# Two-layer graph network on one core: attention probabilities turned by transposing DMA transfers instead of TensorE transposes, with a new bank table and a new order of the work

## The chip, the cores and the metric

The kernel runs on one core of a Trainium2 chip. The time is device microseconds (us) from one launch to its end. Three runs of the kernel before gave 1729.15, 1730.36 and 1730.51 us, so the median is 1730.36 us. All times below are in us unless marked ns.

## The reference, cut to what matters

The input is 64 graphs of 128 nodes with 384 features each, and a weighted adjacency matrix per graph. Two residual blocks follow each other. Everything is float32.

```python
h = maximum(layernorm(x), 0)
# block 1: attention with 12 heads of 32 features, adj added twice to the scores
q, k, v = h @ Wq.T, h @ Wk.T, h @ Wv.T + bv             # per head
scores = einsum('bqhd,bkhd->bhqk', q, k) * 384**-0.5 + (adj + adj)
scores = where(any(scores != 0, -1), scores, -inf)
p = nan_to_num(softmax(scores))
x = x + einsum('bhqk,bkhd->bqhd', p, v) @ Wo.T + bo
# block 2: two layers of a gated graph convolution on h = maximum(layernorm(x), 0)
u = (h @ (h@Wl.T).T) * triu(adj) / sqrt(384) + (h @ (h@Wr.T).T) / sqrt(384) * triu(adj, 1).T
d = exp(u) * adj;  h = relu(layer_norm(d / sum(d) @ (h @ Wlin.T + b)))
x = x + h
```

## The kernel before, in words

Two graphs form a group, so there are 32 groups (`g`, NG = 32) and 256 tokens in a group. Every operand of a large product is kept as a high part and a low part (`HI`, `LO`); a product of two such operands is three matmuls. The high part is written by ScalarE (`hi`, line 480) when it drains a PSUM bank, and the low part by VectorE (`lo`, line 592), which subtracts the high part from the same bank.

The work of a group is cut into named jobs. For the attention: `T1a/T1b` turn the normed input, `QK0..2` and `V0/V1` project, `S{j}{c}` computes the scores of graph `j` for the four heads of chunk `c`, `x{j}{c}` is the exponential, `P{j}{c}` turns the probabilities, `PV{j}` multiplies them with the values, `OT{j}` turns the result and `WO{j}` is the output projection. For the graph layers `l` = 0, 1: `T2a/T2b`, `N{l}{k}` and `HL{l}{j}` project, `U{l}` is the pair product, `C{l}{j}` the aggregation, `HTa/HTb` turn the hidden state between the layers, and `AT` turns the adjacency matrix. There is one table `ORDER` with a fixed list of steps for each engine (lines 82 to 110), run once per turn of the loop. The number beside a step says how many groups ahead it works, so that a turn mixes steps of several groups. `BANK` (lines 71 to 80) says which of the 8 PSUM banks a job fills. Each engine runs its list strictly in order; waits on semaphores (`wait_filled`, `wait_drained`) tie the lists together.

The part that changes is the way of the probabilities. Before, VectorE adds the adjacency to the scores and takes the row maximum in one instruction per head (line 655), writes minus twice the maximum (`m{j}{c}`, line 662), and ScalarE takes the exponential into `prob` (line 509). TensorE then turns four heads into a bank (line 420), ScalarE writes the high part of `pT` (float16) from the bank and VectorE the low part (line 597). `PV` (line 413) reads `pT` as its stationary operand. Before, `prob` has room for both graphs of a group; `pT` has room for one graph.

q and k are restacked through SyncE's DMA queue (line 301): 12 transfers for q and 12 for k in each turn. The masks of the two triangles come from products with constant triangles: the left one on VectorE from the bank of `AT` (line 705), the right one on GpSimd (line 836). GpSimd also applies the last scale and shift of the output (`za`, `zb`, lines 840 and 843) and adds the bias `bo` (`xbo`, line 832). VectorE's step `U{l}` is a chain: `m` multiplies with the masks (line 721), `w` adds the two sides (line 724), `d` multiplies with the turned adjacency (line 727), `dh` and `dl` split (lines 730 and 733), and `C{l}{j}` on TensorE waits for `dl`.

Of the kernel before, what the change touches and what calls it, by code (L numbers as in the profile page):

```python
# [61 lines left out]
def w_lin(l):  # L62
# [9 lines left out]
    0: ["QK2", "N11", "HL11", "C10", "N01", "P10"],  # L72
    1: ["PV1", "OT1", "V0", "U1", "S12", "P01", "P11"],
    2: ["T1b", "QK0", "T2b", "S02", "S11", "P02", "AT"],
    3: ["C01", "HTb", "V1", "P00", "U0"],
    4: ["WO0", "HTa", "N12", "T2a", "S00", "N00", "P12"],
    5: ["WO1", "S10", "HL00"],
    6: ["OT0", "T1a", "QK1", "HL10", "N02", "PV0"],
    7: ["HL01", "C00", "N10", "S01", "C11"],
# [4 lines left out]
        ("out", -2), ("q3", 1), ("ld_x", 2), ("k3", 1), ("ld_adj", 2)],  # L84
# [6 lines left out]
    "ACT": [  # L91
# [6 lines left out]
    "DVE": [  # L98
# [9 lines left out]
    "POOL": [  # L108
        ("za", -2), ("zb", -2), ("xbo", 1), ("gn0", -1), ("ln2", 0), ("ln1", 2), ("ml", 0), ("gn1", -1)],
# [3 lines left out]
SPLIT_JOBS = (["T1a", "T1b", "QK0", "QK1", "QK2", "V0", "V1"] + [f"P{j}{c}" for j in range(G) for c in range(C)] +  # L113
              ["OT0", "OT1", "T2a", "T2b", "AT"] + [f"N{l}{k}" for l in range(L) for k in range(3)] +
# [6 lines left out]
def build(nc, x_d, adj_d, w_d, bias_d, bo_d, lna_d, lnb_d, out_d):  # L121
# [17 lines left out]
    with ExitStack() as ctx:  # L139
# [13 lines left out]
        upper = sb("upper", [P, P])  # L153
        lower = sb("lower", [P, P])
# [16 lines left out]
        prob = sb("prob", [P, G, NH, P])  # L171
# [4 lines left out]
        rmax = sb("rmax", [P, G, NH])  # L176
        nmax = sb("nmax", [P, G, NH])
# [47 lines left out]
        s_mr = sem("mask_right")  # L225
# [7 lines left out]
        s_za, s_zb, s_y = sem("scaled"), sem("shifted"), sem("result")  # L233
# [107 lines left out]
        def _(pe):  # L341
# [39 lines left out]
            def run(step, g):  # L381
# [24 lines left out]
                elif step[:2] == "PV":  # L406
                    j = int(step[2])
                    wait_drained(pe, f"V{j}", g)
                    for c in range(C):
                        wait_drained(pe, f"P{j}{c}", g)  # L410
# [63 lines left out]
        def _(act):  # L474
# [12 lines left out]
            def run(step, g):  # L487
# [17 lines left out]
                elif step[0] == "x" and len(step) == 3:  # L505
                    j, c = int(step[1]), int(step[2])
                    act.wait_ge(s_max[j][c], g + 1)
# [3 lines left out]
                elif step[0] == "P":  # L511
                    j, c = int(step[1]), int(step[2])
# [363 lines left out]
```

## Time and profile before

| what | value |
|---|---|
| median of 3 runs | 1730.36 us |
| the profiled execution itself | 1729.59 us |
| its span, first to last instruction | 1727.8 us |
| TensorE busy | 1590.1 us (92%) |
| VectorE busy | 1283.4 us (74%) |
| ScalarE busy | 922.7 us (53%) |
| GpSimd busy | 450.8 us (26%) |
| mean granted TensorE clock | 0.966 |
| chain that ended last | TensorE 50%, VectorE 26%, ScalarE 13% |

Busy time is an average over the whole span. TensorE is busy in nearly all of it, yet VectorE and ScalarE are on half of the chain that ended last, because the lists of the four engines wait for each other several times in a turn. Which engine limits a stretch has to be read from that stretch.

### The profile page before, as it was taken

To read this page: it belongs to the slowest core of one execution; us is meant where nothing else is said; L and a number is where in the kernel's file an instruction comes from. 1 tells how busy PE (TensorE), PEld (TensorE's weight loads), DVE (VectorE), ACT (ScalarE), POOL (GpSimd) and SP (SyncE) were. 2 spreads that over 40 slices of the span, in tenths; PEclk is the share of its full clock that TensorE was granted. 3 is DMA by queue.
4 is the path that set the end of the run, shared out by engine and by line. 5 is a ranking of instruction groups with operands and counts; after the bars stand their busy time and mean duration, and the time that the engine had idled before them with its cause. 6 is when DMAs were issued, how large, how long until landed. Compare 5 with 4: busy or idle time off the path is not lost.

```text
span 1727.8 us, 39233 instructions
## 1 busy us (share of the span) xinstructions
PE 1590.1 (92%) x13888; PEld 1542.7 (89%) x13888; DVE 1283.4 (74%) x4495; ACT 922.7 (53%) x2155; POOL 450.8 (26%) x804
## 2 busy tenths in 40 slices
PE   4699999999999999999999999999999999999974
PEld 3599999999999999999999999999999999999974
DVE  5567877778887778787777887777788777787752
ACT  3455565455556456556455555545565645555531
POOL 4112321222222232222132232123222223223121
PEclk8799999999999999999999999999999999999996
DMA  6111111211112111111111111111111112111100
GB/s 202 38 36 26 43 41 47 50 49 29 36 41 50 47 50 41 28 45 41 47 50 47 29 39 41 50 47 50 38 30 45 41 47 50 44 29 41 29 10 18
DMA packets 116767, 76.16 MB, mean 44 GB/s; under 512 B 14282, under 2 KB 116432, under 8 KB 116576
## 3 DMA queue, kind: packets, MB, share of 16 engines
q1 hardware_dynamic: 116128, 73.06, 16.6%
q8 instruction: 114, 1.87, 0.5%
q14 instruction: 77, 0.63, 0.1%
q0 software_dynamic: 448, 0.60, 0.1%
HBM read 23.28 MB, written 12.58 MB: 21 GB/s over the span
## 4 chain that ended last, share of the span: by engine, by line
PE 50%; DVE 26%; ACT 13%; issue 6%; SPq 4%; DMA 1%; POOL 1%; POOLq 0%; ACTq 0%; DVEq 0%
PE bank L344 45%; ACT prob L509 6%; DVE prob L655 6%; SPq L301 4%; DVE pT L597 3%; DVE dT L730 3%; DVE work L724 3%; ACT pT L485 3%; ACT n L485 3%; DVE hl L597 2%; PE bank L350 2%; ACT c_sb L541 2%; DVE work L721 1%; DVE stats_gnn L630 1%; DVE rmax L655 1%
## 5 line engine op out<-in xcount | busy, mean ns | idle before, releaser
L344 PE MATMUL bank<-h,weights 128*128 128x256 f32 x3456 | 438.4, 284 | 5.8 <-DVE h L746 5.1
L344 PEld LDWEIGHTS bank<-h,weights 128*128 128x128 f32 x3456 | 420.3, 190 | 6.9 <-issue 5.7
L509 ACT ACTIVATE prob<-prob,nmax 128x128 f32<-128x128 f32 x768 | 236.2, 405 | 71.0 <-DVE nmax L662 71.0
L344 PE MATMUL bank<-hA,weights 128*128 128x256 f32 x1728 | 228.7, 292 | 1.5 <-DVE hA L597 1.5
L344 PEld LDWEIGHTS bank<-hA,weights 128*128 128x128 f32 x1728 | 223.6, 201 | 2.0 <-issue 2.0
L344 PE MATMUL bank<-weights,h 128*128 128x384 f32 x1152 | 224.6, 339 | 0.0
L597 DVE TENSOR_TENSOR n<-bank,n 128x512 fp32r<-128x512 f32 x192 | 131.4, 685 | 113.9 <-ACT n L485 113.7
L485 ACT ACTIVATE qk<-bank 128x512 f16<-128x512 f32 x96 | 57.3, 597 | 270.0 <-PE bank L344 269.9
L344 PEld LDWEIGHTS bank<-weights,h 128*128 128x128 f32 x1152 | 195.6, 188 | 0.0
L485 ACT ACTIVATE n<-bank 128x512 fp32r<-128x512 f32 x192 | 116.3, 606 | 120.2 <-PE bank L344 120.2
L655 DVE CUSTOM_DVE_ANT_0 prob<-bank,adj_sb 128x128 f32<-128x128 f32 x768 | 174.0, 287 | 0.9 <-issue 0.8
L812 POOL TENSOR_SCALAR less_mean_gnn<-mv_gnn 128x2 f32<-128x2 f32 x64 | 14.1, 220 | 556.7 <-DVE mv_gnn L602 556.7
L344 PE MATMUL bank<-n,h 128*128 128x256 f32 x1152 | 153.6, 287 | 0.0
L344 PE MATMUL bank<-hl,dT 128*128 128x386 f32 x384 | 91.2, 377 | 63.2 <-DVE dT L733 60.9
L344 PEld LDWEIGHTS bank<-n,h 128*128 128x128 f32 x1152 | 141.9, 191 | 0.2 <-issue 0.2
L799 POOL TENSOR_SCALAR less_mean_ln<-mv_ln 128x2 f32<-128x2 f32 x64 | 14.1, 220 | 481.0 <-DVE mv_ln L602 481.0
L485 ACT ACTIVATE hl<-bank 128x384 fp32r<-128x384 f32 x128 | 63.9, 499 | 141.1 <-PE bank L344 141.1
L597 DVE TENSOR_TENSOR pT<-bank,pT 128x512 f16<-128x512 f32 x192 | 126.0, 684 | 14.0 <-ACT pT L485 13.2
L344 PEld LDWEIGHTS bank<-hl,dT 128*128 128x128 f32 x384 | 70.2, 204 | 72.4 <-issue 72.4
L344 PE MATMUL bank<-weights,hA 128*128 128x384 f32 x576 | 115.2, 344 | 2.7 <-DVEq L587 2.7
L344 PE MATMUL bank<-weights,oT 128*128 128x384 f32 x576 | 115.9, 346 | 1.8 <-DVE oT L597 1.8
L420 PE MATMUL bank<-ident,prob 128*128 128x128 f32 x768 | 109.2, 280 | 1.8 <-ACT prob L509 1.7
(112 smaller groups left out, 2874.6 us busy)
## 6 DMA issues: line engine op xcount, KB each, us to landing
q<-qk SPq DMA_DIRECT2D x384, 48.0 KB, 1.9
k<-qk SPq DMA_DIRECT2D x384, 48.0 KB, 2.0
x_sb<-x SPq DMA_DIRECT2D x32, 384.0 KB, 3.5
out<-x SPq DMA_DIRECT2D x32, 384.0 KB, 2.5
adj_sb<-adj SPq DMA_DIRECT2D x32, 128.0 KB, 2.1
prob<-w SPq DMA_DIRECT2D x4, 576.0 KB, 6.4
x<-w SPq DMA_DIRECT2D x3, 576.0 KB, 4.6
pT<-w SPq DMA_DIRECT2D x3, 576.0 KB, 6.1
```

The lines of the kernel that those rows point to most:

```text
L301: sp.dma_start(dst[D * r:D * r + D, a:NH:HC, :], qk[D * a:D * a + D, part, first:first + C, :]).then_inc(s, 16)
L344: mm = pe.matmul(out, lhsT, rhs, start=(n == 0), stop=(n == len(pairs) - 1))
L350: mm = pe.transpose(bank(job)[:, n * T + j * P:n * T + (j + 1) * P], src[:, j, c * P:(c + 1) * P], ident[:, :])
L420: mm = pe.transpose(bank(step)[:, a * P:(a + 1) * P], prob[:, j, c * HC + a, :], ident[:, :])
L485: act.activation(out, src, ACT.Copy).then_inc(s_hi, 1)
L509: e = act.activation(prob[:, j, h, :], prob[:, j, h, :], ACT.Exp, bias=nmax[:, j, h:h + 1], scale=2.0)
L541: act.activation(c_sb[:, j, :], bank(f"C1{j}")[:, 0:H], ACT.Copy).then_inc(free(f"C1{j}"), 1)
L597: dve.tensor_tensor(out, src, hi_part if hi_part.dtype == F16 else hi_part.bitcast(F32), ALU.subtract).then_inc(free(job), 1)
L630: dve.bn_stats(stats["gnn"][:, j, :], bank(f"C{l}{j}")[:, 0:H]).then_inc(s_gst[l][j], 1)
L655: r = dve.tensor_tensor_reduce(prob[:, j, h, :], bank(step)[:, a * P:(a + 1) * P], adj_sb[:, p, j, :], 1.0, -3.0e38, ALU.add, ALU.max, rma ...
L724: dve.tensor_tensor(wu, tu[:, :, 0, :], tu[:, :, 1, :], ALU.add).then_inc(s_w[l], 1)
L730: dve.tensor_copy(dT[:, HI, :, :], wu).then_inc(s_dhi[l], 1)
```

## The change

1. The `P` jobs leave TensorE. ScalarE copies `prob` from SBUF into a new float16 tile `pp` (named `prob_parts` in the profile; steps `ph`), VectorE writes the low part (`pl`), and 12 transposing DMA transfers per turn on SyncE's queue write `pT` from it (steps `pth` and `ptl`: high and low, graph `j`, chunk `c`). `prob` now has room for one graph only, and `pp` as well.
2. The row maximum is taken as a minimum of minus twice the sum, so that the `m` steps go.
3. `AT` is drained by ScalarE alone, and both masks are made on GpSimd by `affine_select` (steps `mu`, `ml`).
4. `za`, `zb`, `xbo` and `y` are cut into one step per graph.
5. `BANK` and `ORDER` are new. The loop now runs up to three groups ahead instead of two.

```diff
 BANK = {
-    0: ["QK2", "N11", "HL11", "C10", "N01", "P10"],
+    0: ["C00", "S02", "S01", "N01"],
...
     "SP": [
-        ("out", -2), ("q3", 1), ("ld_x", 2), ("k3", 1), ("ld_adj", 2)],
+        ("pth12", 1), ("ptl12", 1), ("ptl11", 1), ("pth11", 1), ("pth10", 1), ("ptl10", 1), ("ld_adj", 2), ("out", -1),
+        ("q3", 2), ("ld_x", 3), ("k3", 2), ("pth02", 2), ("ptl02", 2), ("pth00", 2), ("pth01", 2), ("ptl01", 2), ("ptl00", 2)],
...
-        prob = sb("prob", [P, G, NH, P])
+        prob = sb("prob", [P, NH, P])
+        pp = sb("prob_parts", [P, 2, NH, P], F16)
         pT = sb("pT", [P, 2, NH, P], F16)
...
+                elif step[:2] == "pt":
+                    part, j, c = "hl".index(step[2]), int(step[3]), int(step[4])
+                    hs = slice(c * HC, (c + 1) * HC)
...
+                    sp.wait_ge(s_part[part][c], G * g + j + 1)
+                    if j == 0:
+                        wait_filled(sp, "PV1", g - 1)
+                    else:
+                        wait_filled(sp, "PV0", g)
+                    sp.dma_start_transpose(pT[:, part, hs, :], pp[:, part, hs, :].rearrange("p h q -> p (h q)")).then_inc(s_turned[part][c], 16)
...
                 elif step[:2] == "PV":
...
-                    for c in range(C):
-                        wait_drained(pe, f"P{j}{c}", g)
+                    for part in (HI, LO):
+                        for c in range(C):
+                            pe.wait_ge(s_turned[part][c], 16 * (G * g + j + 1))
...
-                elif step[0] == "P":
-                    j, c = int(step[1]), int(step[2])
-                    pe.wait_ge(s_exp[j][c], g + 1)
-                    for a in range(HC):
-                        mm = pe.transpose(bank(step)[:, a * P:(a + 1) * P], prob[:, j, c * HC + a, :], ident[:, :])
...
-                        e = act.activation(prob[:, j, h, :], prob[:, j, h, :], ACT.Exp, bias=nmax[:, j, h:h + 1], scale=2.0)
+                        e = act.activation(prob[:, h, :], prob[:, h, :], ACT.Exp, bias=rmin[:, j, h:h + 1], scale=-1.0)
...
+                elif step[:2] == "ph":
...
+                    act.wait_ge(s_exp[j][c], g + 1)
+                    ge(act, s_turned[HI][c], 16 * (G * g + j))
+                    act.activation(pp[:, HI, hs, :], prob[:, hs, :], ACT.Copy).then_inc(s_part[HI][c], 1)
...
-                        r = dve.tensor_tensor_reduce(prob[:, j, h, :], bank(step)[:, a * P:(a + 1) * P], adj_sb[:, p, j, :],
-                                                     1.0, -3.0e38, ALU.add, ALU.max, rmax[:, j, h:h + 1])
+                        r = dve.tensor_tensor_reduce(prob[:, h, :], bank(step)[:, a * P:(a + 1) * P], adj_sb[:, p, j, :],
+                                                     -2.0, 3.0e38, ALU.add, ALU.min, rmin[:, j, h:h + 1])
...
-                    dve.tensor_scalar(nmax[:, j, hs], rmax[:, j, hs], -2.0, None, ALU.mult).then_inc(s_max[j][c], 1)
...
+                elif step[:2] == "pl":
...
+                    dve.wait_ge(s_part[HI][c], G * g + j + 1)
+                    ge(dve, s_turned[LO][c], 16 * (G * g + j))
+                    dve.tensor_tensor(pp[:, LO, hs, :], prob[:, hs, :], pp[:, HI, hs, :], ALU.subtract).then_inc(s_part[LO][c], 1)
...
-                    dve.tensor_tensor(mask[:, :, 0, :], bank("AT")[:, 0:T].rearrange("p (g i) -> p g i", g=G),
-                                      upper[:, :].unsqueeze(1).to_broadcast([P, G, P]), ALU.mult).then_inc(free("AT"), 1)
...
+                elif step == "mu":
...
+                    pool.affine_select(out=mask[:, :, 0, :], in_=adjT[:, :, :], compare_op=ALU.is_ge, fill=0.0, base=0,
+                                       pattern=[[0, G], [-1, P]], channel_multiplier=1).then_inc(s_mask[0], 1)
```

TensorE, from the last scores of a turn to the first pair product `U0` (`n2,h0`), before. Rows with `ident,prob` are the `P` jobs, `v2,pT` is `PV0`, `ident,adj_sb` is `AT`:

```order
L404 MATMUL bank5<-k3,q3 128x128 x4
L420 MATMUL bank1<-ident,prob 128x128 x4
L420 MATMUL bank2<-ident,prob 128x128 x4
L344 MATMUL bank0<-h0,weights 128x256 x18
L344 MATMUL bank5<-weights,h0 128x384 x9
L344 MATMUL bank5<-bias_rows,pick 128x384
L413 MATMUL bank6<-v2,pT 128x33 x36
L420 MATMUL bank1<-ident,prob 128x128 x4
L438 MATMUL bank2<-ident,adj_sb 128x128 x2
L420 MATMUL bank4<-ident,prob 128x128 x4
L420 MATMUL bank0<-ident,prob 128x128 x4
L344 MATMUL bank3<-n2,h0 128x256 x18
```

And now, up to the row ahead of the second `v2,pT` (`ident,o_sb` is `OT0`, the second `weights,h0` is `HL01`, `ident,qk` is `T1a` and `T1b`, `weights,oT` is `WO0`):

```order
L416 MATMUL bank1<-k3,q3 128x128 x4
L356 MATMUL bank3<-weights,h0 128x384 x9
L356 MATMUL bank3<-bias_rows,pick 128x384
L426 MATMUL bank5<-v2,pT 128x33 x36
L445 MATMUL bank1<-ident,adj_sb 128x128 x2
L356 MATMUL bank6<-n2,h0 128x256 x18
L433 MATMUL bank2<-ident,o_sb 128x128 x3
L356 MATMUL bank4<-weights,h0 128x384 x9
L356 MATMUL bank4<-bias_rows,pick 128x384
L362 MATMUL bank6<-ident,qk 128x128 x4
L362 MATMUL bank7<-ident,qk 128x128 x2
L356 MATMUL bank1<-weights,oT 128x384 x9
```

The row behind it is `L426 MATMUL bank3<-v2,pT 128x33 x36`, `PV1`. The `P` jobs are gone, `HL00` (`weights,h0`) still stands before `PV0`, and between `U0` and `PV1` there are now `T1a`, `T1b` and `WO0` as well, which stood behind `PV1`.

The order of SyncE's DMA queue over one turn, with what each row waits for, before (`full` and `free` are the filled and drained counts of a bank):

```order
L301 DMA q3<-qk 32x3x256 [waits full2,full1,full5,free6,free2,full7,full4]
L301 DMA q3<-qk 32x3x256 x11
L308 DMA x_sb<-x 128x2x384 [waits free5,free4]
L301 DMA k3<-qk 32x3x256 [waits full2,full1,full5,free6,free0,full7,full4]
L301 DMA k3<-qk 32x3x256 x11
L315 DMA adj_sb<-adj 128x2x128 [waits free2,free1,free5,full2,mask_right,free7,free4]
L329 DMA out<-x1 128x2x384 [waits result]
```

And now, where `full3` is the bank of `PV1` and `full5` the bank of `PV0`:

```order
L300 DMA k3<-qk 32x3x256 x11
L337 DMA_TRANSPOSE pT<-prob_parts 128x4x128 [waits full3,prob_hi2]
L337 DMA_TRANSPOSE pT<-prob_parts 128x4x128 [waits full3,prob_lo2]
L337 DMA_TRANSPOSE pT<-prob_parts 128x4x128 [waits full3,prob_hi0]
L337 DMA_TRANSPOSE pT<-prob_parts 128x4x128 [waits full3,prob_hi1]
L337 DMA_TRANSPOSE pT<-prob_parts 128x4x128 [waits full3,prob_lo1]
L337 DMA_TRANSPOSE pT<-prob_parts 128x4x128 [waits full3,prob_lo0]
L337 DMA_TRANSPOSE pT<-prob_parts 128x4x128 [waits full5,prob_hi2]
L337 DMA_TRANSPOSE pT<-prob_parts 128x4x128 [waits full5,prob_lo2]
```

Four more transposing transfers with `full5` follow, and then `ld_adj`. So the six transfers of the second graph can start only when TensorE has finished `PV0`, and the six of the first graph only when it has finished `PV1` of the group before.

## Rows read from the trace of the kernel before

**Rows 1.** TensorE's waits, whole run: engine, line, releaser; total, times, longest.
```profile
PE bank L344 <- DVE dT L733: 60.9, 31, 4.1
```
**Rows 2.** Windows: length, then busy by engine, PEclk, DMA share, GB/s.
```profile
802.17:854.26 52.09, 49.99 (x437) 48.69 (x435) 39.77 (x141) 28.37 (x68) 13.64 (x24) 0.97 0.16 41
852.00:864.00 12.00, 12.00 (x119) 11.61 (x116) 11.53 (x76) 9.89 (x29) 0.00 (x0) 1.00 0.01 2
823.90:826.00 2.10, 2.09 (x7) 2.10 (x8) 2.10 (x6) 0.00 (x0) 0.00 (x0) 0.53 0.03 8
```
**Rows 3.** Timeline of TensorE: first scores of four turns (start, length).
```profile
134.06 0.62 PE L404 MATMUL bank<-k,q 96*128 96x128 f16 x8
...
851.64 0.62 PE L404 MATMUL bank<-k,q 96*128 96x128 f16 x8
...
1055.06 0.62 PE L404 MATMUL bank<-k,q 96*128 96x128 f16 x8
...
1107.13 0.62 PE L404 MATMUL bank<-k,q 96*128 96x128 f16 x8
```
**Rows 4.** Timeline of TensorE from the P jobs to PV1, one turn.
```profile
857.11 0.61 PE L420 MATMUL bank<-ident,prob 128*128 128x128 f32 x4
857.48 1.30 PE L344 MATMUL bank<-hl,dT 128*128 128x386 f32 x6
...
858.85 1.04 PE L420 MATMUL bank<-ident,prob 128*128 128x128 f32 x8
859.65 2.38 PE L344 MATMUL bank<-h,weights 128*128 128x256 f32 x18
...
863.61 1.07 PE L413 MATMUL bank<-v,pT 128*128 128x33 f16 x36
864.53 0.64 PE L420 MATMUL bank<-ident,prob 128*128 128x128 f32 x4
...
866.01 2.40 PE L344 MATMUL bank<-n,h 128*128 128x256 f32 x18
...
870.32 1.07 PE L413 MATMUL bank<-v,pT 128*128 128x33 f16 x36
```
**Rows 5.** Timeline of TensorE behind PV1, an early turn.
```profile
104.83 1.07 PE L413 MATMUL bank<-v,pT 128*128 128x33 f16 x36
105.75 0.85 PE L350 MATMUL bank<-ident,qk 128*128 128x128 f32 x6
106.36 1.83 PE L344 MATMUL bank<-weights,oT 128*128 128x384 f32 x9
108.03 1.21 PE L344 MATMUL bank<-hl,dT 128*128 128x386 f32 x6
```
**Rows 6.** Timeline of ScalarE: exponentials, then a copy of four heads.
```profile
854.12 3.63 ACT L509 ACTIVATE prob<-prob,nmax 128x128 f32<-128x128 f32 x12 [1.49 <-DVE nmax L662]
857.76 0.60 ACT L485 ACTIVATE pT<-bank 128x512 f16<-128x512 f32 x1
```
**Rows 7.** Timeline of VectorE: two additions of U's chain, the last split before U0.
```profile
817.53 1.68 DVE L724 TENSOR_TENSOR work<-work 128x256 f32<-128x256 f32 x1
...
850.90 0.42 DVE L724 TENSOR_TENSOR work<-work 128x256 f32<-128x256 f32 x1
...
864.10 0.69 DVE L597 TENSOR_TENSOR n<-bank,n 128x512 fp32r<-128x512 f32 x1
```
**Rows 8.** Timeline of SyncE's queue: start, length.
```profile
813.46 0.37 SPq L315 DMA_DIRECT2D adj_sb<-adj  x1
...
832.83 7.66 SPq L301 DMA_DIRECT2D q<-qk  x12
```
**Rows 9.** DMA: a queue with its packets; an issue with us to landing.
```profile
q1 hardware_dynamic: 116128, 73.06, 16.6%
q<-qk SPq DMA_DIRECT2D x384, 48.0 KB, 1.9
```
**Rows 10.** Timeline of GpSimd: scale, shift and bias of the output.
```profile
817.10 1.84 POOL L840 TENSOR_TENSOR c_sb<-c_sb,lna_all 128x768 f32<-128x768 f32 x1 [2.44 <-ACT c_sb L552]
```

More of the change, by code:

```diff
@@ L71 @@
 BANK = {
-    0: ["QK2", "N11", "HL11", "C10", "N01", "P10"],
[L73 to L79, printed above, removed]
+    0: ["C00", "S02", "S01", "N01"],
+    1: ["AT", "WO0", "HTa", "V0", "HL10", "S00", "S12", "S10"],
+    2: ["OT0", "QK0", "N10", "N00"],
+    3: ["PV1", "OT1", "WO1", "U1", "C11", "HL00"],
+    4: ["HL01", "QK1", "V1", "HL11", "C10"],
+    5: ["C01", "T2a", "S11", "PV0"],
+    6: ["U0", "T1a", "HTb", "N11"],
+    7: ["T1b", "QK2", "N12", "T2b", "N02"],
 }
@@ L83 @@
     "SP": [
-        ("out", -2), ("q3", 1), ("ld_x", 2), ("k3", 1), ("ld_adj", 2)],
[2 rows of a table added]
     "PE": [
[5 rows of a table removed]
-    "ACT": [
[6 rows of a table removed]
-    "DVE": [
[9 rows of a table removed]
[4 rows of a table added]
+    "ACT": [
[6 rows of a table added]
+    "DVE": [
[8 rows of a table added]
     "POOL": [
-        ("za", -2), ("zb", -2), ("xbo", 1), ("gn0", -1), ("ln2", 0), ("ln1", 2), ("ml", 0), ("gn1", -1)],
-}
-SPLIT_JOBS = (["T1a", "T1b", "QK0", "QK1", "QK2", "V0", "V1"] + [f"P{j}{c}" for j in range(G) for c in range(C)] +
-              ["OT0", "OT1", "T2a", "T2b", "AT"] + [f"N{l}{k}" for l in range(L) for k in range(3)] +
+        ("mu", 0), ("za1", -1), ("za0", -1), ("zb1", -1), ("zb0", -1), ("xbo0", 2), ("gn0", 0), ("xbo1", 2), ("ln2", 1),
+        ("ml", 1), ("ln1", 3), ("gn1", 0)],
+}
+SPLIT_JOBS = (["T1a", "T1b", "QK0", "QK1", "QK2", "V0", "V1",
+              "OT0", "OT1", "T2a", "T2b"] + [f"N{l}{k}" for l in range(L) for k in range(3)] +
               [f"HL{l}{j}" for l in range(L) for j in range(G)])
@@ L215, in build @@
         s_xn2 = [sem(f"xn2_{j}") for j in range(G)]
-        s_xbo = sem("x_plus_bo")
+        s_xbo = [sem(f"x_plus_bo{j}") for j in range(G)]
         s_q3, s_k3 = sem("q3_in"), sem("k3_in")
-        s_max = [[sem(f"row_max{j}{c}") for c in range(C)] for j in range(G)]
         s_exp = [[sem(f"exps{j}{c}") for c in range(C)] for j in range(G)]
+        s_part = [[sem(f"prob_{n}{c}") for c in range(C)] for n in ("hi", "lo")]
+        s_turned = [[sem(f"prob_turned_{n}{c}") for c in range(C)] for n in ("hi", "lo")]
         s_stats = {k: sem(f"stats_{k}") for k in ("ln1", "ln2")}
@@ L232, in build @@
         s_h1lo = {ab: sem(f"h1_lo_{ab}") for ab in "ab"}
-        s_za, s_zb, s_y = sem("scaled"), sem("shifted"), sem("result")
+        s_za, s_zb, s_y = ([sem(f"{n}{j}") for j in range(G)] for n in ("scaled", "shifted", "result"))
         s_out = [sem("out0"), sem("out1")]
@@ L243, in build @@
         SPLIT_AFTER = {
-            "ACT": {"": (0,), "xn1_1": (1,), "T1a": (2, 3), "QK0": (4, 5), "QK1": (6,), "QK2": (7,), "V0": (8,), "V1": (9,)},
-            "DVE": {"ln1_ag": (0,), "T1a": (1, 2), "QK0": (3, 4), "QK1": (5,), "QK2": (6, 7), "V0": (8,), "V1": (9,)}}
+            "ACT": {"": (0,), "xn1_1": (1,), "T1b": (2, 3), "QK0": (4, 5), "QK1": (6,), "QK2": (7,), "V0": (8,), "V1": (9,)},
+            "DVE": {"ln1_ag": (0,), "T1b": (1, 2), "QK0": (3, 4), "QK1": (5,), "QK2": (6, 7), "V0": (8,), "V1": (9,)}}
         def staged(m):
-            prob_flat = prob[:, :, :, :].rearrange("p g h q -> p (g h q)")
             flat = (x1[:, :, :, :].rearrange("p k g h -> p (k g h)")[:, 0:C * H],
                     pT[:, :, :, :].rearrange("p s h q -> p (s h q)").bitcast(F32)[:, 0:C * H],
-                    prob_flat[:, 0:C * H], prob_flat[:, NH * P:NH * P + C * H])[STAGE_OF[m]]
+                    prob[:, :, :].rearrange("p h q -> p (h q)")[:, 0:C * H],
+                    pp[:, :, :, :].rearrange("p s h q -> p (s h q)").bitcast(F32)[:, 0:C * H])[STAGE_OF[m]]
             return flat.rearrange("p (c o) -> p c o", c=C)
@@ L526, in run @@
                     ge(act, s_d[1], g)
-                    hi(step, g, adjT[:, :, :], T, "p (g i) -> p g i", g=G)
+                    wait_filled(act, "AT", g)
+                    act.activation(adjT[:, :, :], bank("AT")[:, 0:T].rearrange("p (g i) -> p g i", g=G), ACT.Copy).then_inc(free("AT"), 1)
                 elif step[0] == "N":
@@ L717, in run @@
                     if step[3:] == "m":
-                        wait_drained(dve, "AT", g)
-                        dve.wait_ge(s_mr, g + 1)
+                        for side in range(2):
+                            dve.wait_ge(s_mask[side], g + 1)
                         wait_filled(dve, job, g)
@@ L733, in run @@
                         dve.tensor_tensor(dT[:, LO, :, :], wu, dT[:, HI, :, :].bitcast(F32), ALU.subtract).then_inc(s_dlo[l], 1)
[L734 to L737 removed]
+                elif step[0] == "y":
+                    j = int(step[1])
+                    dve.wait_ge(s_zb[j], g + 1)
+                    dve.scalar_tensor_tensor(out=x1[:, p, j, :], in0=c_sb[:, j, :], scalar=0.0, in1=x1[:, p, j, :],
+                                             op0=ALU.max, op1=ALU.add).then_inc(s_y[j], 1)
                 elif step[:2] == "HT":
@@ L828, in run @@
                     gnn_scale(int(step[2]), g)
-                elif step == "xbo":
-                    for j in range(G):
-                        pool.wait_ge(s_xn1[j], g + 1)
-                    pool.tensor_tensor(x_sb[:, p, :, :], x_sb[:, p, :, :], bo_all[:, :].unsqueeze(1).to_broadcast([P, G, H]), ALU.add).then_inc(s_xbo, 1)
+                elif step[:3] == "xbo":
+                    j = int(step[3])
+                    pool.wait_ge(s_xn1[j], g + 1)
+                    pool.tensor_tensor(x_sb[:, p, j, :], x_sb[:, p, j, :], bo_all[:, :], ALU.add).then_inc(s_xbo[j], 1)
+                elif step == "mu":
+                    wait_drained(pool, "AT", g)
+                    wait_drained(pool, "U1", g - 1)
+                    pool.affine_select(out=mask[:, :, 0, :], in_=adjT[:, :, :], compare_op=ALU.is_ge, fill=0.0, base=0,
+                                       pattern=[[0, G], [-1, P]], channel_multiplier=1).then_inc(s_mask[0], 1)
                 elif step == "ml":
@@ L835, in run @@
                     wait_drained(pool, "U1", g - 1)
-                    pool.tensor_tensor(mask[:, :, 1, :], adj_sb[:, p, :, :], lower[:, :].unsqueeze(1).to_broadcast([P, G, P]), ALU.mult).then_inc(s_mr, 1)
-                elif step == "za":
-                    for j in range(G):
-                        pool.wait_ge(s_z[j], g + 1)
-                    pool.tensor_tensor(c_sb[:, :, :], c_sb[:, :, :], lna_all[:, :].unsqueeze(1).to_broadcast([P, G, H]), ALU.mult).then_inc(s_za, 1)
-                elif step == "zb":
-                    pool.wait_ge(s_za, g + 1)
-                    pool.tensor_tensor(c_sb[:, :, :], c_sb[:, :, :], lnb_all[:, :].unsqueeze(1).to_broadcast([P, G, H]), ALU.add).then_inc(s_zb, 1)
+                    pool.affine_select(out=mask[:, :, 1, :], in_=adj_sb[:, p, :, :], compare_op=ALU.is_ge, fill=0.0, base=-1,
+                                       pattern=[[0, G], [1, P]], channel_multiplier=-1).then_inc(s_mask[1], 1)
+                elif step[:2] == "za":
+                    j = int(step[2])
+                    pool.wait_ge(s_z[j], g + 1)
+                    pool.tensor_tensor(c_sb[:, j, :], c_sb[:, j, :], lna_all[:, :], ALU.mult).then_inc(s_za[j], 1)
+                elif step[:2] == "zb":
+                    j = int(step[2])
+                    pool.wait_ge(s_za[j], g + 1)
+                    pool.tensor_tensor(c_sb[:, j, :], c_sb[:, j, :], lnb_all[:, :], ALU.add).then_inc(s_zb[j], 1)
             for step, g in program("POOL"):
```

55 lines of the change are left out of this document (18 added, 37 removed), and 38 rows, old and new, of the table ORDER.

## The prediction

> **What bounds the kernel now.** I read the windows first. In a turn of 52.09 us TensorE is busy 49.99, VectorE 39.77 [rows 2], so TensorE comes first. Then its waits: all that counts is one wait a turn, 31 times, 60.9 us in all, for the last step of VectorE's chain `U0` (`dl`) [rows 1], some 1.95 us each. The starts of the first scores show the turns: 14 turns from 134.06 to 851.64, so 51.26 us on average, and one of 52.07 [rows 3]. A turn of 52.07 has a slow stretch behind that wait: from 823.90 on the granted clock is 0.53, half of full speed, that is 1.2 GHz against 2.4, after TensorE stood idle [rows 2]. If such turns alternate with others, the others take 2 x 51.26 - 52.07 = 50.45 us, and the drop costs 1.6.
>
> Third, the windows by stage. From 852 to 864, the stretch of the scores and the `P` jobs, VectorE is busy 11.53 of 12.00 us [rows 2]. TensorE shows 12.00 there too, but work taken from TensorE alone in this stretch uncovers VectorE at once. Fourth, VectorE's timeline: the same addition of 256 columns takes 1.68 us at 817.53 and 0.42 at 850.90 [rows 7]. At the first place GpSimd runs its scaling, 1.84 us from 817.10 [rows 10].
>
> The Trainium skill has a rule for this (SBUF — State Buffer, "SBUF: two separate sides", on the shared port pair): a VectorE instruction with two SBUF inputs and a GpSimd instruction that reads SBUF exclude each other. By that rule, the trace agrees: 1.68 against 0.42. The rule speaks against this change, because each new `pl` has two SBUF inputs where the old low part read a bank.
>
> **What goes from TensorE.** From the first scores of a turn to `PV0` are 863.61 - 851.64 = 11.97 us [rows 3, 4]. In it the four turnings take 857.48 - 857.11 = 0.37 and the eight 859.65 - 858.85 = 0.80. Between `PV0` and `U0` stand 14 turnings in 866.01 - 864.53 = 1.48 us, 12 of them `P`: 1.27 [rows 4]. Together 2.44 us a turn, 78 us over 32 turns. That is the gain if TensorE bounds all along and nothing new waits.
>
> What is left for TensorE in a turn of the new order, without any wait:
> - first scores to `PV0`: 11.97 - 0.37 - 0.80 = 10.80.
> - `PV0` to `PV1`: 870.32 - 863.61 - 1.27 = 5.44 as before; the new order puts `T1` (106.36 - 105.75 = 0.61) and `WO0` (108.03 - 106.36 = 1.67) [rows 5] in front of `PV1` too, so 7.72.
> - `PV1` to the next first scores: 134.06 - 104.83 = 29.23 [rows 3, 5], less the same 0.61 and 1.67, so 26.95.
>
> Sum 45.5 us. With `U0`'s wait and the slow clock gone as well, this is the floor.
>
> **What goes and comes on the others.** VectorE: the low parts stay six per turn at 512 columns; I price `pl` as the old one, 0.69 us as for the split of that size [rows 7], at most 1.68 - 0.42 = 1.26 more where GpSimd holds it up. In the scores' stretch there now stand four of them where three stood, against six small `m` steps removed; I take that as even. Then VectorE still finishes the last split ahead of `U0` at 864.10 + 0.69 - 851.64 = 13.2 us after the first scores [rows 3, 7], while TensorE, without `P` jobs, would start `U0` at about 10.80 + 0.92 (864.53 - 863.61) + 0.21 for `AT` = 11.9. So 1.3 of the 2.44 us turn into a wait for VectorE, and the floor is 46.8, say 47. The product for the left mask moves to GpSimd and `za`, `zb`, `xbo`, `y` are only cut in two: nothing of them is on this path, GpSimd being busy 13.64 of 52.09 [rows 2]. If that cover is gone they cost up to a microsecond or so a turn; I price it at 0 to 1.
>
> **The new wait.** This is the term that decides. Six transposing transfers fill `pT` for the first graph, then `PV0`; only when TensorE has filled `PV0`'s bank may the next six start, then `PV1`. They sit on one queue and run in order. Let t be the time that one occupies the queue, and t + 1.3 from the issue of the last to its landing (the q copies: 1.9 to landing, of which 7.66 / 12 = 0.64 is the issue [rows 8, 9]). The first can be issued when eight exponentials and one copy are done: the 12 take 3.63 us and the copy 0.60 [rows 6], so 2.4 + 0.6 behind the first exponential, which I put 1.5 after the first scores, earlier than today's 854.12 - 851.64 = 2.5, since it no longer waits for the second chunk and `m`. That is 4.5. Then:
> - `PV0` starts at 4.5 + 5t + t + 1.3 = 5.8 + 6t, if that is over 10.8.
> - `PV1` starts at that + 0.92 + 6t + 1.3 = 8.0 + 12t.
> - the turn is 26.95 more: 35.0 + 12t, if that is over 47.
>
> Behind the waiting `PV1` stand `QK0`, `C01`, `C00` and `QK1` on TensorE, and on VectorE `PV1.r` stands ahead of `dh` and `dl`, which `C01` needs: nothing passes it. On the queue `q3` waits for `QK1` anyway, so it is not delayed further; it moves with `PV1`.
>
> The trace shows no transposing transfer, so t is bounded by the nearest rows. Each moves 128 x 512 float16, 128 KB. Low: the adjacency load, also 128 KB, occupies the queue 0.37 us [rows 8]. High: a q copy has 96 rows of 512 bytes in 0.64 us; a transposing transfer reads 512 rows of 256 bytes, at the same rate 3.4 us. Between them: by the mean packet of the queue, 0.166 x 16 x 1727.8 / 116128 = 39.5 ns [rows 9], 512 packets over 16 engines take 1.26 us; by bytes, q copies move 48 KB in 0.64 us, so 128 KB take 1.7 us. I take 1.7: the q copies are the nearest row, SBUF to SBUF, float16 and on the same queue. It gives `PV0` at 16.0 (5.2 us of waiting), `PV1` at 28.4 where TensorE is free at 16.0 + 7.72 = 23.7 (4.7 us), and a turn of 55.4. Both waits are longer than the one that lets the clock fall today; at 1.6 a drop, 0 to 3.2 a turn, I take 1.7. Turn: 57.1.
>
> The Trainium skill (Advanced Engine Details and Errata, "X-Bar Transpose (TRN2)") says that transposing transfers are as fast as regular ones. No run here shows it yet. By it t would be the issue time, the fast case below. Another page (VectorE: DVE Perf Modes, "The three transpose paths") gives 1309 ns for one 128x128 block; four of them one behind the other would be an estimate of 5.2 us, and a turn of 97.
>
> **Sum.** The ends of the run stay: 1727.8 - 31 x 51.26 = 139 us. 31 x 57.1 + 139 = 1909, and 1.8 around the span gives 1911. The profiled execution of before (1729.59) lies 0.8 under the median, nothing here. I forecast 1910 us, 10% slower.
>
> **Rivals.**
> - *The transfers are hidden* (t up to 1.0; the other side). The turn is 47 to 47.5: 31 x 47.3 + 141 = 1607, 7% faster. For it: a load of the same bytes occupies the queue 0.37 us, and the 16 engines are 84% idle [rows 2]. The page on transposes as fast as copies says the same. Against it: the q copies need 0.64 for 48 KB. It decides below t = 1.3, where 35.0 + 12t with some of the clock's price meets 51.26. 25%.
> - *Nearly even, gaining a little or nothing* (t of 1.0 to 1.35, the estimate by packets): at 1.26 the turn is 50.1, with one clock drop in part 51: 31 x 51 + 141 = 1722. 15%.
> - *By rows* (t over 2.75): at 3.4 the turn is 75.8 + 1.7 = 77.5, the time 2544. The 256-byte rows speak for it; that 12 such transfers would be 41 us of the queue beside 15 for the copies, for a chip with idle engines, speaks against. 17%.
> - *VectorE and GpSimd exclude each other on all six `pl`*: 6 x 1.26 = 7.6 us more VectorE work per turn, of which the waiting of TensorE hides most. `mu` starts only after `pl11` and `pl10`, so it touches at most one or two: 1 to 2.5 us a turn, 31 to 78 us on top of any case. Inside the ranges.
>
> **The numbers.** t of 1.35 to 2.75: 43%, my forecast, 1730 to 2300. With 25, 15 and 17 for the others, faster by over 0.2% (which is about what a measurement of this kernel tells from no change) is the first rival and most of the second: 37%; within 0.2%: 3%; slower: 60%. The range of 8 in 10 goes from 1600 (the turn of 47, nothing lost elsewhere) to 2300 (t = 2.75).
>
> **What would show it.** The duration of `DMA_TRANSPOSE` on the queue and its landing are t and t + 1.3; the turns follow as 35 + 12t. TensorE's longest waits must be at the two `v,pT` groups, released by DMA, near 5 us each, 32 times. TensorE's busy time must fall by about 78 us, unless the clock gives it back. `U0`'s wait for `dl` must be gone. If instead the waits at `v,pT` are missing, t is under 1 and the time near 1610. I am wrong in kind if the transfers are quick and yet the time grows, or if the wait stands at the scores for k.

## The result: 3.5% slower, and the profile after

The changed kernel takes 1789.23 us (median of 4 runs, 1785.5 to 1799.98) against 1730.43 us for the kernel before. The ratio is 1.0351, 95% interval 1.0306 to 1.0396. The forecast was 1910 us with a range of 1600 to 2300: the direction is right and the time lies in the range, but the loss is a third of the one forecast. The profiled execution took 1790.44 us, with a span of 1788.7. Times below are medians too; of the four executions in the last experiment one took 6279.17 us and is left out.

TensorE's waits over the whole run, in the columns of [rows 1]:

```profile
PE bank L426 <- DMA pT<-prob_parts: 149.0, 62, 6.9
PE bank L416 <- DMA k<-qk: 26.8, 17, 9.9
PE bank L356 <- ACT c_sb L552: 21.4, 30, 1.0
...
PE bank L356 <- DVE dT L738: 2.9, 1, 2.9
```

The wait for the last step of `U0` (60.9 us before) is gone. In its place stands one for the transposing transfers, 149 us in 62 pieces: 88.7 us ahead of `PV0` and 60.3 ahead of `PV1`. The profile's section on busy time, and one turn in a window (columns as in [rows 2]):

```profile
PE 1535.7 (86%) x13120; PEld 1491.2 (83%) x13120; DVE 1171.9 (66%) x4303; ACT 924.0 (52%) x2155; POOL 484.6 (27%) x928
...
776.11:827.53 51.42, 46.94 (x410) 45.82 (x411) 35.33 (x134) 28.11 (x67) 14.88 (x28) 0.97 0.32 73
```

TensorE is 54 us less busy and VectorE 111 us less. For TensorE I had announced 78 less unless the clock gives it back; the mean granted clock is 0.940, where it was 0.966. The turn shown is the quickest. Over 29 turns from 143.74 to 1678.22 (rows like those of [rows 3]) the mean is 52.91, and single turns take 51.4 to 55.2, where the turns before alternated between about 50.5 and 52.1. The timeline of TensorE in the turn behind it, from the first scores to the job behind `PV1`:

```profile
827.53 0.62 PE L416 MATMUL bank<-k,q 96*128 96x128 f16 x8
...
841.49 1.16 PE L426 MATMUL bank<-v,pT 128*128 128x33 f16 x36 [2.20 <-DMA pT<-prob_parts]
842.49 0.67 PE L445 MATMUL bank<-ident,adj_sb 128*128 128x128 f32 x2
842.81 3.41 PE L356 MATMUL bank<-n,h 128*128 128x256 f32 x18
...
852.13 1.06 PE L426 MATMUL bank<-v,pT 128*128 128x33 f16 x36 [1.59 <-DMA pT<-prob_parts]
853.04 2.36 PE L356 MATMUL bank<-hA,weights 128*128 128x256 f32 x18
```

Both `PV` jobs wait for their transfers, 2.20 and 1.59 us. `U0` (`n,h`) takes 3.41 us, where the same job took 2.40 [rows 4]: the clock fell in the wait. The windows of `U0` and of the job behind `PV1` show a mean granted clock of 0.66 and 1.00 (the third figure from the end of each line):

```profile
842.81:846.22 3.41, 3.41 (x22) 3.41 (x21) 2.04 (x6) 2.19 (x5) 2.32 (x3) 0.66 0.38 77
...
853.04:855.40 2.36, 2.36 (x26) 2.36 (x22) 1.75 (x7) 0.00 (x0) 0.00 (x0) 1.00 0.03 10
```

On SyncE's queue (start, length), and as a summary of all transposing transfers (shortest, median and longest, then landing):

```profile
832.12 18.34 SPq L337 DMA_TRANSPOSE pT<-prob_parts  x12
...
L337 SPq DMA_TRANSPOSE pT<-prob_parts x384: 1188/1217/2350, 44.3 to 1700.7; - x192
...
DMA to landing us min/median/max: 2.4/2.4/4.7
```

One transfer holds the queue 1.22 us in the median, the next starts about 1.3 us after it, and it lands 2.4 us after its issue. The addition of `U0`'s chain, which took 1.68 us beside GpSimd [rows 7], is back to its short time in 26 of 32 turns; in the other six it takes 1.30 us, beside GpSimd's addition of `bo`:

```profile
848.61 0.41 DVE L729 TENSOR_TENSOR work<-work 128x256 f32<-128x256 f32 x1
```

### The profile page after: what moved, and what is told of

It is laid out like the page before. It is cut to its first block and busy times, and to the rows that moved or that the text cites. A ratio compares the mean times of both kernels' runs of the same rounds, so it can differ in the third digit from the quotient of the medians.

```text
span 1788.7 us, 38712 instructions
## 1 busy us (share of the span) xinstructions
PE 1535.7 (86%) x13120; PEld 1491.2 (83%) x13120; DVE 1171.9 (66%) x4303; ACT 924.0 (52%) x2155; POOL 484.6 (27%) x928
## 5 line engine op out<-in xcount | busy, mean ns | idle before, releaser
L356 PE MATMUL bank<-h,weights 128*128 128x256 f32 x3456 | 427.3, 281 | 5.1 <-DVE h L752 5.1
L516 ACT ACTIVATE prob<-prob,rmin 128x128 f32<-128x128 f32 x768 | 238.4, 394 | 50.0 <-DVE rmin L667 50.0
L356 PE MATMUL bank<-hA,weights 128*128 128x256 f32 x1728 | 236.2, 293 | 1.4 <-DVE hA L608 1.4
L426 PEld LDWEIGHTS bank<-v,pT 128*128 128x128 f16 x2304 | 64.8, 98 | 168.8 <-issue 168.8
L426 PE MATMUL bank<-v,pT 128*128 128x33 f16 x2304 | 69.7, 180 | 150.1 <-DMA pT<-prob_parts 149.0
L356 PE MATMUL bank<-n,h 128*128 128x256 f32 x1152 | 183.5, 323 | 0.0
L356 PEld LDWEIGHTS bank<-n,h 128*128 128x128 f32 x1152 | 171.7, 229 | 0.2 <-issue 0.2
L492 ACT ACTIVATE n<-bank 128x512 fp32r<-128x512 f32 x192 | 110.4, 593 | 107.3 <-PE bank L356 107.3
L699 DVE TENSOR_TENSOR prob_parts<-prob,prob_parts 128x512 f16<-128x512 f32 x192 | 134.8, 716 | 1.2 <-ACT prob_parts L523 1.2
L523 ACT ACTIVATE prob_parts<-prob 128x512 f16<-128x512 f32 x192 | 112.5, 619 | 0.1
```

The source lines that it names most:

```text
L356: mm = pe.matmul(out, lhsT, rhs, start=(n == 0), stop=(n == len(pairs) - 1))
L426: mm = pe.matmul(bank(step)[:, h * DA:(h + 1) * DA], pT[:, a, h, :], v2[:, b, j, h, :], start=(h == 0 and n == 0), stop=(n == 2), skip_gro ...
L492: act.activation(out, src, ACT.Copy).then_inc(s_hi, 1)
L516: e = act.activation(prob[:, h, :], prob[:, h, :], ACT.Exp, bias=rmin[:, j, h:h + 1], scale=-1.0)
L523: act.activation(pp[:, HI, hs, :], prob[:, hs, :], ACT.Copy).then_inc(s_part[HI][c], 1)
L699: dve.tensor_tensor(pp[:, LO, hs, :], prob[:, hs, :], pp[:, HI, hs, :], ALU.subtract).then_inc(s_part[LO][c], 1)
```

## The experiments

The question was where 149 us of waiting come from, how much the rest of the change is worth, what sets the 1.22 us, and what the clock costs. Code is cut to the lines that matter; `...` marks what is left out of a line.

### The transfers alone

Transfers of a constant tile on SyncE's queue, and none of the network. `blocks` is 4, 1 and 2 in six transfers each, then 12 in three; the plain copies move 128 rows of 512 columns, six times.

```diff
+sp.dma_start_transpose(dst[name][:, k, 0:blocks * P].rearrange("p (h q) -> p h q", h=blocks), src[:, 0:blocks * P]).then_inc(s, 16)
...
+sp.dma_start(dst[name][0:rows, k, 0:cols], src[0:rows, 0:cols]).then_inc(s, 16)
```

> Only transfers on SyncE's queue, none of the network: the output is a plain copy of x. It measures t by itself: transposing transfers inside SBUF of 128x512 float16 (four 128x128 blocks) alone and six in a row, of 128x128, of 128x256 and of 128x1536, then plain copies of 128x512 and of 32 rows of 3072 bytes. Theory A (the queue makes descriptors for every block): the issue grows with the blocks, about 0.3 us per block over a small fixed part, so 0.4 to 0.6 us for one block, 0.7 to 0.9 for two, 1.2 for four, 3.5 for twelve. Theory B (a fixed price per transposing instruction): 1.2 us for one block as for four, and little more for twelve. A plain copy of the same 128 KB should occupy the queue 0.4 us under both.

The queue's timeline shows the first of the six transfers of four blocks, the first of one block and the first of two:

```profile
9.48 1.19 SPq L36 DMA_TRANSPOSE turn_b2b<-src  x1
...
18.50 1.13 SPq L36 DMA_TRANSPOSE turn_b2b<-src  x1
...
27.23 1.19 SPq L36 DMA_TRANSPOSE turn_b2b<-src  x1
```

And the summaries, of all 18 of these, of the three of twelve blocks and of the plain copies of 128 KB:

```profile
L36 SPq DMA_TRANSPOSE turn_b2b<-src x18: 1131/1239/1267, 9.5 to 33.6; - x18
...
L36 SPq DMA_TRANSPOSE turn_big<-src x3: 1440/1799/1800, 36.1 to 39.5; - x3
...
L48 SPq DMA_DIRECT2D copy_b2b<-src x6: 578/601/602, 43.6 to 46.8; - x6
```

Theory B holds. A transposing transfer holds the queue 1.13 to 1.27 us whether it turns one, two or four blocks, and twelve blocks take 1.44 to 1.80, where the DMA share from 36 to 43 us was 0.90. A plain copy of four blocks' bytes takes 0.60, where I had expected 0.4. My theory A, a price per block, is refuted: twelve blocks in one transfer cost half as much as in three.

### Plain copies in place of the turning

```diff
-sp.dma_start_transpose(pT[:, part, hs, :], pp[:, part, hs, :].rearrange("p h q -> p (h q)"))
+sp.dma_start(pT[:, part, hs, :], pp[:, part, hs, :])
```

> The changed kernel with plain copies in place of the transposing transfers, same bytes, same waits, same order; the probabilities are not turned, so this leaves the turning out. Theory A (t decides the time, by turn = max(47, 35 + 12t)): t falls from 1.22 to about 0.4, the waits of TensorE at the v,pT groups vanish or fall under 0.5 us, the turn is 47 to 48.5, the time 1610 to 1650 us. Theory B (what costs is the round trip of the landing and the handshake, not t): the waits stay over 1 us each and the time over 1720.

The probabilities reach `PV` unturned here. 1635.9 us (median of 4), ratio to before 0.9462 (0.9444 to 0.948). TensorE's waits and the transfers:

```profile
PE bank L356 <- DVE n L608: 17.7, 26, 0.8
PE bank L426 <- DMA pT<-prob_parts: 7.0, 9, 3.4
...
L337 SPq DMA_DIRECT2D pT<-prob_parts x384: 464/540/1650, 44.5 to 1545.7; - x192
```

With 0.54 us in place of 1.22 the waits go from 149.0 to 7.0 us, and the mean turn is 48.1. Theory A. The wait for `n` is the one that the prediction puts at `U0`, VectorE being late with the last split: 0.7 us in 26 of the turns, where it says 1.3.

### No waiting for pT

```diff
-for part in (HI, LO):
-    for c in range(C):
-        pe.wait_ge(s_turned[part][c], 16 * (G * g + j + 1))
...
-mm = pe.matmul(..., pT[:, a, h, :], v2[:, b, j, h, :], ...)
+mm = pe.matmul(..., fixed[:, :], v2[:, b, j, h, :], ...)
```

> The changed kernel with all its transfers still issued and landing, but TensorE multiplies with a constant tile instead of pT and so waits for no transfer; the product with the probabilities is left out. Theory A (the waits for pT are the whole loss): turn 47 to 48, time 1600 to 1640 us. Theory B (the new order itself, the k transfers behind the queue or the contention of VectorE and GpSimd cost a good part): over 1690 us, with other waits in place of those for pT.

1639.21 us, ratio 0.9478 (0.9459 to 0.9497), mean turn 48.2. The twelve transposing transfers still run (384 of 1.22 us in the median), and the time is within 4 us of the kernel with plain copies: what they do to the queue and the DMA engines costs next to nothing as long as nobody waits for them. TensorE's waiting for them makes the whole difference of 150 us to the changed kernel. The rest of the change, new order and turnings gone from TensorE, is worth 5.2%, or 91 us. No run separates its parts; by the prediction's rows the turnings alone are 78.

### A second place for pT

```diff
-    wait_filled(sp, "PV0", g)
-sp.dma_start_transpose(pT[:, part, hs, :], ...)
+    for cc in range(C):
+        wait_filled(sp, f"S1{cc}", g); wait_filled(sp, f"S0{cc}", g)
+    wait_filled(sp, "PV1", g - 1)
+sp.dma_start_transpose(pTs[j][:, part, hs, :], ...)     # pTs[1] is q3's memory; step q3 also waits for PV1 of g - 1
```

> The changed kernel, result unchanged, with the turned probabilities of the second graph of a group written over q3 (dead once the scores of the group are done), so its six transfers wait for the last scores and not for PV0. Theory A (the chain PV0, then six transfers, then PV1 makes PV1's wait): PV1's wait of 1.2 to 3 us goes to under 0.5, PV0's of 2.2 to 3.3 stays; the turn falls from 52.9 by 1.5 to 3 us, the time is 1695 to 1745 us. Theory B (PV1 is bound by the last low part, written by VectorE behind PV0's division, or by the queue being full): the wait stays over 1 us and the time within 1% of 1789.

1743.4 us, ratio 1.0086 (1.0054 to 1.0118), mean turn 51.4, 1.5 less. `PV0`'s and `PV1`'s waits:

```profile
PE bank L432 <- DMA pT<-prob_parts: 88.9, 32, 6.9
...
PE bank L432 <- DMA q<-prob_parts: 20.2, 20, 2.1
```

`PV1` now waits 20.2 us in the run instead of 60.3, and `PV0` 88.9 as before. This is theory A, at the upper end of its time and with 0.6 us a turn left at `PV1`, where it says under 0.5: about 46 us of the loss are `PV1`'s chain.

### Fewer and more transfers

Three kernels move the same bytes with 8, 4 and 24 transposing transfers a turn instead of 12.

```diff
# 8 a turn (e4); 4 a turn (e5) has one span of all three chunks
-("pth12", 1), ("ptl12", 1), ("ptl11", 1), ("pth11", 1), ("pth10", 1), ("ptl10", 1), ...
+("pth12", 1), ("ptl12", 1), ("pth1b", 1), ("ptl1b", 1), ...     # b: chunks 0 and 1 in one transfer
# 24 a turn (e6)
+for half in range(2):
+    hh = slice(c * HC + 2 * half, c * HC + 2 * half + 2)
+    sp.dma_start_transpose(pT[:, part, hh, :], pp[:, part, hh, :].rearrange("p h q -> p (h q)"))
```

> The changed kernel, result unchanged, with the transfers of chunks 0 and 1 issued as one of eight blocks (128x1024): 8 transposing transfers a turn instead of 12, same bytes. In the run of transfers alone one occupies the queue 1.2 us whether it turns one, two or four blocks, and 1.44 to 1.80 at twelve. Theory A (the number of instructions on the queue makes the wait): the last for the first graph is issued 8.7 us after the first scores, when its low part is ready, and lands at about 12; PV0's wait falls from 2.2-3.3 to under 1 us and PV1's to under 0.7, and the clock drops mostly go; turn 48 to 49, time 1640 to 1680, faster than the kernel before. Theory B (the blocks or bytes count): the waits stay as they are and the time near 1789.

> As e4_merged_8, with all three chunks in one transfer of twelve blocks: 4 a turn. The queue is nearly idle, but prob_parts has room for one graph, so the split of chunk 2 of the second graph now waits for the landing of all of the first graph's low parts, about 12.8 us after the first scores, 2 us later than VectorE comes to it. Theory A: VectorE waits there, U0 starts 1 to 2 us later for it; time 1660 to 1710, between e4_merged_8 and the kernel before. Theory B (only the count of transfers counts): as fast as e4_merged_8 or faster.

> The changed kernel, result unchanged, with every transposing transfer cut into two of two heads (two blocks): 24 a turn, same bytes. Theory A (a fixed 1.28 us from one to the next): each step of the chain takes twice the time; by 35 + 12t with t = 2.56 the turn is 65.7, with clock drops 67, the time 2190 to 2290 us. Theory B (time by bytes or blocks): the time stays within 3% of 1789.

| transfers a turn | mean turn | time | ratio to before (interval) | waits for pT, whole run |
|---|---|---|---|---|
| 4 | 51.1 | 1728.0 | 0.9993 (0.998 to 1.0007) | 50.4 |
| 8 | 49.4 | 1671.66 | 0.9667 (0.964 to 0.9694) | 53.1 |
| 12 | 52.9 | 1789.23 | 1.0351 (1.0306 to 1.0396) | 149.0 |
| 24 | 69.0 | 2304.54 | 1.3328 (1.3305 to 1.3351) | 611.2 |

The summaries for 8 and for 24, and for 4 what took the transfers' place, VectorE's wait and TensorE's:

```profile
L340 SPq DMA_TRANSPOSE pT<-prob_parts x256: 1188/1246/2571, 44.5 to 1590.1; - x128
```
```profile
L339 SPq DMA_TRANSPOSE pT<-prob_parts x768: 1167/1236/2541, 44.5 to 2213.6; - x192
```
```profile
DVE prob_parts L702 <- DMA pT<-prob_parts: 65.3, 32, 3.2
...
PE bank L359 <- DVE n L611: 39.2, 31, 1.8
```

The count of transfers decides, not the bytes. With two blocks in each instead of four a transfer takes the same 1.24 us, and the kernel with 24 takes 29% more time than the one with 12. The transfers of eight blocks take 1.25 us in the median. Four a turn is worse than eight, for the reason written before: `prob_parts` comes free only with the landing of the one big transfer, VectorE waits 65 us in its split of chunk 2, and `U0` behind it 39. The clock adds to it: `U0` takes 3.57 us in the mean, 2.60 with eight transfers, and `PV1` waits only 0.6 us in the whole run, so no wait behind `U0` covers the slower job. The run with 24 came out a little over the 2190 to 2290 expected, and the one with 4 at 1728 a little over 1660 to 1710.

### Eight transfers and the second place together

> e4_merged_8 with the second graph's turned probabilities written over q3, as in e3_second_pT; result unchanged. In e4_merged_8 what is left is PV1's wait (1.8 us in the turn read, 53 us for both groups in the run), because its four transfers of 1.2 us and the landing of 3.1 start only behind PV0. Theory A (that chain is the rest of the loss): both waits under 0.5 us, turn 48.1 to 48.6 like the kernel with plain copies, time 1635 to 1655. Theory B (the rest of PV1's wait is the low part of chunk 0, which VectorE writes behind PV0's division): PV1 still waits over 1 us and the time is within 1% of 1672.

1644.89 us, ratio 0.951 (0.9495 to 0.9526), mean turn 48.3, with nothing left out: faster than both kernels. The wait for pT over the whole run, and TensorE in one turn, the two `PV` jobs (`v,pT` and `v,q`) with `U0` between them:

```profile
PE bank L435 <- DMA pT<-prob_parts: 39.0, 32, 5.2
...
728.70 1.06 PE L435 MATMUL bank<-v,pT 128*128 128x33 f16 x36 [0.40 <-DMA pT<-prob_parts]
...
730.22 2.38 PE L365 MATMUL bank<-n,h 128*128 128x256 f32 x18 [0.20 <-DVE n L617]
...
737.30 1.07 PE L435 MATMUL bank<-v,q 128*128 128x33 f16 x36
```

`PV1` no longer waits, and all but 9 us of the gap to the kernel with plain copies is closed. The time and the turn are theory A's. Its waits are not: `PV0` waits 0.40 us in the turn shown, but 1.1 in the median and 39.0 in the run, where it says under 0.5. Most of that costs no time: with plain copies `PV0` starts 11.7 us after the first scores and `PV1` 9.0 behind it, here 12.8 and 8.2, since part of what is lost at `PV0` is waiting for VectorE at `U0` otherwise.

### TensorE kept busy while it waits

```diff
 # ahead of PV's waits: 20 before PV0 and 12 before PV1 (e7); 14 before PV0 alone (e9)
+for _ in range(...):
+    pe.transpose(bank(step)[:, 0:P], ident[:, :], ident[:, :])
```

> The changed kernel, result unchanged, with TensorE turning the identity into the waiting bank 20 times before PV0 and 12 times before PV1, about 2.1 and 1.2 us of work in the place of idling. The transfers are not touched. Theory A (after each wait the granted clock falls to 1.2 GHz for a while, which costs about 1.5 us a turn): clock share from 0.94 to over 0.97, turn 51.3 to 52.2, time 1735 to 1770. Theory B (the clock drops cost nothing, since the chain through the transfers sets the pace anyway): the time stays within 0.7% of 1789, or grows where the filling outlasts the wait.

> The changed kernel, result unchanged, with TensorE turning the identity 14 times (about 1.5 us) before PV0 only, less than PV0 ever waits, so it can't outlast the wait. U0 behind PV0 took 3.4 us instead of 2.4 in the changed kernel, the clock having fallen. Theory A (that time is hidden, since PV1 waits for transfers that count from PV0's end): U0 goes back to 2.4 us, PV1's wait grows by as much, the time stays within 1% of 1789. Theory B (the clock drop is paid): the time falls by 25 to 40 us, to 1750 to 1765.

Both are slower than the changed kernel: 1816.94 (ratio to before 1.0514, 1.0499 to 1.0529) and 1823.18 (1.054, 1.0519 to 1.0561), both outside the times of theory A. One turn of the second, then the windows of `U0` and `QK0` with the granted clock (1.00 and 0.64):

```profile
807.53 1.69 PE L422 MATMUL bank<-ident 128*128 128x128 f32 x14
810.67 1.06 PE L428 MATMUL bank<-v,pT 128*128 128x33 f16 x36 [1.44 <-DMA pT<-prob_parts]
...
811.75 2.40 PE L356 MATMUL bank<-n,h 128*128 128x256 f32 x18
...
821.14 1.06 PE L428 MATMUL bank<-v,pT 128*128 128x33 f16 x36 [2.68 <-DMA pT<-prob_parts]
822.04 3.40 PE L356 MATMUL bank<-hA,weights 128*128 128x256 f32 x18
...
811.75:814.15 2.40, 2.40 (x22) 2.40 (x22) 2.28 (x6) 2.06 (x4) 1.41 (x3) 1.00 0.27 55
...
822.04:825.44 3.40, 3.40 (x26) 3.40 (x22) 2.32 (x8) 0.00 (x0) 0.00 (x0) 0.64 0.12 42
```

`U0` is back to 2.40 us and `PV1`'s wait has grown by about as much, 1.59 to 2.68 (60.3 to 97.4 in the whole run), as theory A of e9 says. But then the clock falls in that longer wait, and `QK0` behind `PV1` takes 3.40 us instead of 2.36, where nothing hides it. Counting the jobs of 18 matmuls that took over 3 us between 150 and 1650: in the changed kernel 22 of `U0` and 8 of `QK`, here 3 and 24. The mean turn is 54.05 us, 1.1 longer, and 0.9 of that lies between `PV1` and the next first scores (28.64 against 27.72). So the clock drop was hidden behind `PV0` and is paid behind `PV1`; neither theory had foreseen that filling one wait moves the drop to the other. For e7 the same count is 0 and 14, which goes the same way, but there all three stretches of the turn grew by 0.2 to 0.3 us, the one ahead of `PV0` too, where in part of the turns the filling left nothing or under 0.2 us of the wait; this fits the growth that theory B of e7 allows where the filling outlasts the wait, but what its 28 us are made of stays open.

## Why the prediction was wrong in size

**What bounds the kernel: right; the floor: 1.1 us too low.** The wait for `dl` is gone and a small one for VectorE at `U0` came, as forecast. Without waits for pT the turn is 48.1 to 48.2 (e1, e2), not 47. Most of the difference lies ahead of `PV0`, which in e1 starts 11.7 us after the first scores instead of 10.8: `HL00` waits 0.7 us a turn for ScalarE's `c_sb`, a wait that the new order brought and my sum has at nothing. In the changed kernel it is covered by the wait for pT.

**The chain and its formula: right.** The first transfer was put 4.5 us after the first scores; it started at 832.12 - 827.53 = 4.6. `PV0` was put at 5.8 + 6t and `PV1` at 8.0 + 12t. With the 1.3 us from start to start these give 13.6 and 23.6; the turn shown has 14.0 and 24.6, since `PV` starts 0.35 us behind the landing in both places, which the formula leaves out. The wait stands at both `v,pT` groups, released by DMA.

**The step that failed: "I take 1.7: the q copies are the nearest row".** t is 1.22 us, 1.3 from start to start. I scaled the bytes of plain copies. The transfers alone show that neither bytes nor blocks set it up to four blocks, and the kernel with 8 transfers shows 1.25 us for eight: it is a price per transposing instruction, 1.13 to 1.27 us, twice that of a plain copy of the same size (0.60). The bound by packets, 1.26, came out near it for a reason that the runs refute. With t = 1.3 my own formula gives 35.0 + 15.6 + 1.7 = 52.3 a turn against 52.9 measured; with 1.7 it gave 57.1. These 4.8 us, over 31 turns 149, are more than the whole miss of 121 (1910 - 1789); the rest goes the other way, 0.6 a turn and the ends of the run, 1788.7 - 31 x 52.91 = 148 us instead of 139. Those 9 us are the first two turns: they took 43.2 and 49.8 us before, so that 31 turns of 51.26 left too little for the ends, and take 50.8 and 53.5 now. The rival "nearly even" had the right t, and I had given it 15%; it came out slower than even because of those two turns and the 2.3 us a turn by which 52.9 exceeds 35.0 + 15.6. In part these are single transfers of up to 2.35 us (the mean is 1.27, the median 1.22). I have no run on those. What they are stays open; of the four turns under 51.9 none has one over 1.44 us. The waits for k are no part of it: behind the first two turns they sum to 7 us, and they are larger in e1 and e2.

**The waits' size: 2.2 and 1.6 us in the turn shown, not 5.2 and 4.7**, from the same t. In the run the mean is 2.8 and 1.9.

**The clock: wrong place, and too dear.** I charged 1.7 us a turn for drops in both waits. The drop behind `PV0` is free, because `PV1`'s transfers count from `PV0`'s end; only one behind `PV1` is paid (e9). By stages the mean turn has 14.34 us to `PV0`, 10.85 on to `PV1` and 27.72 to the next first scores, where the formula with 1.3 has 13.6, 10.0 and 26.95. In the main only the last 0.8 can be the clock, and with plain copies, where no job behind `PV1` is slow, that stretch takes 27.34 too, so 0.4 is the likelier price. That 52.3 lies so near 52.9 is luck: the 1.7 stood in for the starts behind the landings and for the long transfers.

**VectorE and GpSimd excluding each other: small.** `pl` took 0.68 us in the median (626 to 1232 ns), as the old split [rows 7]. Of the 192, 15 took over 0.9 us: all are `pl10`, beside GpSimd's scaling, 8 us in the run by its mean of 0.93 against 0.68. `pl10` is written behind `PV0` and its transfer goes last of six, so it should be off the path; no run tests that. The Trainium skill's rule (SBUF — State Buffer, "SBUF: two separate sides") names this collision, and the 15 slow ones agree with it; in this order it meets one `pl` of six, and that in half of the turns.

**Two other prices for a transposing transfer.** The Trainium skill's statement that transposing transfers are as fast as regular ones (Advanced Engine Details and Errata, "X-Bar Transpose (TRN2)") does not hold here for small ones: 1.2 us of the queue against 0.6, and with twelve blocks 1.8 us for 384 KB, an estimate of 218 GB/s from this run. The 1309 ns per 128x128 block that the Trainium skill gives in "The three transpose paths" (VectorE: DVE Perf Modes) lie between the 1.13 to 1.23 us for which one block holds the queue here and the 2.2 to 2.4 us to its landing. Four in one instruction do not add up to the estimate of 5.2 us.

## What to carry to other kernels

When work is moved to a DMA queue, count the instructions on the queue and not only the bytes. Here a transposing transfer cost 1.2 us of the queue for one block, four or eight, so merging twelve a turn into eight turned a loss of 3.5% into a gain of 3.3%, and a second destination made it 4.9%. Ask of each chained buffer how many transfers stand between the release and the next use, and break the chain or shorten it before giving up the idea. Merging has an end where a larger transfer holds its source longer: four transfers a turn only came out even. For an operation that the trace does not show, a rate per byte is only one of the possible laws; the forecast should keep a fixed price per instruction beside it.

## What was not expected of the hardware

- A transposing transfer has a fixed hold on the queue: 1.13 to 1.23 us for 32 KB, 1.2 to 1.3 for 128 KB, 1.44 to 1.80 for 384 KB, against 0.60 for a plain copy of 128 KB. It lands 2.2 to 2.5 us after its issue up to four blocks, and 3.8 to 4.2 at twelve.
- Keeping TensorE busy in one wait moved the slow clock to the next, longer wait and cost 34 us (1789 to 1823).
